# Other orders within even and odd groups, other bank holding times, and one more rounding on the scalar engine in a fused attention and expert-routing kernel

## The reference

```python
xn = _layernorm(x)
# attention: h = rmsnorm(xn) * scale
q, k, v = (einsum("bsd,dhe->bshe", h, w) for w in (wq, wk, wv))
weights = softmax(einsum("bqhd,bkhd->bhqk", q * 64**-0.5, k))
attn = einsum("bqhe,hed->bqd", einsum("bhqk,bkhd->bqhd", weights, v), w_out) + b_out
# experts
logits = silu(xn @ rw1 + rb1) @ rw2 + rb2          # 512 hidden, 8 experts
k_prob = softmax(top_2(logits))
for e in range(8):
    ffn += we[:, None] * (silu(xn @ w1[e] + b1[e]) @ w2[e] + b2[e])
out = x + attn + ffn
```

## Time and profile before

| | |
|---|---|
| median of 3 runs | 2175.5 us (2175.19 to 2176.46) |
| the profiled execution | 2178.22 us, of which the span from first to last instruction is 2176.4 us |
| PE, DVE, ACT, POOL busy in the span | 92%, 75%, 71%, 43% |
| mean granted TensorE clock | 0.965 |

### The profile page before, as it was taken

How to read it: one execution, slowest core, us unless ns; L and a number is a source line. 1 busy time by engine, 2 the same in 40 slices (tenths; PEclk the granted TensorE clock), 3 DMA queues, 4 the chain that set the end, 5 groups by cost and what they waited for, 6 DMA issues and landing times.

```text
span 2176.4 us, 45192 instructions
## 1 busy us (share of the span) xinstructions
PE 2000.1 (92%) x16646; PEld 1285.2 (59%) x16646; DVE 1628.4 (75%) x2716; ACT 1547.2 (71%) x3654; POOL 945.7 (43%) x790
## 2 busy tenths in 40 slices
PE   7898999989998888999889999999999999999997
PEld 5555555555655555565456666666666666666664
DVE  6777777777876677777667877777877877778785
ACT  5667677766766676676567677777777777777774
POOL 4333454443334443332114544645546445464454
PEclk9999999999999999999999999999999999999999
DMA  2122222221011101101213333433333333333332
GB/s 79 37 62 82 80 96 81 77 71 38 28 37 39 35 27 40 39 22 36 84 51 84 70 84 80 79 80 79 87 77 71 88 78 77 80 79 81 75 74 45
DMA packets 132697, 141.96 MB, mean 65 GB/s; under 512 B 25438, under 2 KB 99038, under 8 KB 132446
## 3 DMA queue, kind: packets, MB, share of 16 engines
q1 hardware_dynamic: 101886, 118.34, 17.4%
q0 software_dynamic: 30592, 20.73, 8.0%
HBM read 102.65 MB, written 38.46 MB: 65 GB/s over the span
## 4 chain that ended last, share of the span: by engine, by line
PE 65%; ACT 11%; DVE 11%; issue 7%; another core or an unknown queue 4%; DMA 1%; POOL 0%; SPq 0%; DVEq 0%; POOLq 0%; ACTq 0%
PE pair L452 17%; PE pair L393 12%; PE pair L423 9%; PE pair L237 7%; PE pair L239 5%; PE pair L238 5%; DVE NM L402 4%; ACT PR L408 3%; DVE ZZ L772 2%; PE pair L498 2%; PE pair L500 2%; ACT ZZ L763 1%; DVE PT L438 1%; ACT PT L435 1%
## 5 line engine op out<-in xcount | busy, mean ns | idle before, releaser
L408 ACT ACTIVATE PR<-pair,NM 128x512 f32<-128x512 f32 x1024 | 710.1, 715 | 54.9 <-DVE NM L402 54.3
L402 DVE TENSOR_REDUCE NM<-pair 128x2 f32<-128x1024 f32 x512 | 610.0, 1211 | 72.5 <-PE pair L393 52.9
L435 ACT COPY PT<-pair 128x512 f32<-128x512 f32 x640 | 357.3, 605 | 370.2 <-PE pair L423 348.1
L393 PE MATMUL pair<-KS,QS 64*128 64x512 f32 x3072 | 507.4, 432 | 77.4 <-DVE KS L378 44.5
L452 PE MATMUL pair<-PT,V 128*64 128x512 f32 x2048 | 476.7, 608 | 5.3 <-ACT PR L408 5.3
L423 PEld LDWEIGHTS pair<-idn,PR 64*128 64x128 f32 x8192 | 348.2, 143 | 143.6 <-issue 33.5
L393 PEld LDWEIGHTS pair<-KS,QS 64*128 64x128 f32 x3072 | 267.1, 192 | 251.9 <-issue 155.7
L423 PE MATMUL pair<-idn,PR 64*128 64x64 f32 x8192 | 354.7, 227 | 56.2 <-ACT HS L557 18.2
L778 POOL TENSOR_TENSOR HH<-ZZ,HH 128x512 fp32r<-128x512 f32 x156 | 226.3, 1493 | 322.9 <-DVE HH L777 166.0
L813 POOL DMA_INDIRECT out<-YS,IDW x156 | 245.7, 1575 | 176.3 <-DVE YS L805 119.3
L452 PEld LDWEIGHTS pair<-PT,V 128*64 128x64 f32 x2048 | 137.8, 139 | 274.8 <-issue 255.7
(11 more groups left out here) (168 smaller groups left out, 2866.7 us busy)
## 6 DMA issues: line engine op xcount, KB each, us to landing
E<-w_tab SPq DMA_DIRECT2D x78, 512.0 KB
RB<-l_rows SPq DMA_DIRECT2D x127, 256.0 KB
XG<-slots SPq DMA_DIRECT2D x39, 264.0 KB, 6.3
w_tab<-SPL SPq DMA_DIRECT2D x16, 512.0 KB, 4.3
l_rows<-RT SPq DMA_DIRECT2D x508, 1.0 KB
xin<-in_x SPq DMA_DIRECT2D x16, 256.0 KB, 7.6
XQ<-in_x SPq DMA_DIRECT2D x16, 256.0 KB, 6.4
RAW<-in_w SPq DMA_DIRECT2D x16, 256.0 KB, 7.7
```

The source lines that it names most:

```text
L393: m = e.matmul(bank[bk + j], a[half[j], cols], c[half[j], :], start=(k == 0), stop=(k == 2))
L402: add("dve", lambda e: e.tensor_reduce(NM[:, 2 * t:2 * t + 2], both[:], AX.X, ALU.max, negate=True), needs=[("S", n, t), *([("exp", n - 1, ...
L408: add("act", lambda e: e.activation(PR[:, k, :], bank[bk], ACT.Exp, bias=NM[:, k:k + 1], accum_out=RS[:, n % 2, j, t:t + 1]), needs=[("max ...
L435: add("act", lambda e, r=r: e.copy(dst[r], src[r]), needs=[("T", n, t), *old], name=("PT", n, t, r), place=f"turn{t % 2}")
```

## The change

Nothing is computed otherwise. Orders, engines, distances and holding times change:

```diff
 PE_ORDER = [
-    "S0 T0 S1 T1 inverse kq spread attend ahead weighted experts route".split(),
-    "S0 T0 S1 spread T1 kq ahead attend experts route inverse weighted".split(),
+    "S0 T0 S1 T1 kq spread attend inverse ahead experts weighted route".split(),
+    "S0 T0 S1 ahead spread T1 kq attend route experts weighted inverse".split(),
 ]
 DVE_ORDER = [
-    "inverse max0 turn0 max1 turn1 low values sums side".split(),
-    "max0 turn0 max1 inverse turn1 sums values low side".split(),
+    "inverse turn0 max0 max1 turn1 low values sums side".split(),
+    "max0 max1 turn1 sums values turn0 inverse low side".split(),
 ]
 ACT_ORDER = [
-    "turn0 exp00 exp01 turn1 high exp10 exp11 values hi side".split(),
-    "turn0 exp00 exp01 high values turn1 exp10 exp11 hi side".split(),
+    "turn0 exp00 exp01 turn1 high exp10 exp11 values side hi".split(),
+    "turn0 exp00 exp01 high turn1 exp10 values side exp11 hi".split(),
 ]
-VALUES_ON = [["dve", "act", "act", "act"], ["dve", "act", "act", "act"]]
-HIGH_ON = ["dve", "dve", "dve", "act"]
+VALUES_ON = [["dve", "act", "act", "act"], ["act", "dve", "act", "act"]]
+HIGH_ON = ["act", "dve", "dve", "act"]
 PLAN = {
-    -5: [("rows",)],
-    -3: [("turn",), ("in",)],
+    -7: [("rows",)],
+    -3: [("in",), ("turn",)],
 HOLD = {
-    "S0": (0.9, 4.6), "S1": (0.7, 6.2), "T": (0.5, 2.5), "kq": (0.8, 1.8), "V": (0.8, 2.2), "PV": (3.6, 1.7),
-    "R": (0.2, 2.3), "OP": (1.7, 0.5), "h1": (0.8, 4.3), "w2": (2.9, 1.9), "xg": (0.5, 3.9), "yT": (0.6, 5.1),
-    "r1": (0.8, 3.7), "hT": (0.6, 0.4), "xT": (0.5, 5.2), "oT": (0.5, 2.6), "other": (0.9, 1.3),
+    "S0": (0.9, 5.2), "S1": (0.7, 6.2), "T": (0.5, 3.1), "kq": (0.8, 1.5), "V": (0.8, 2.2), "PV": (3.6, 2.0),
+    "R": (0.2, 0.1), "OP": (1.7, 1.1), "h1": (0.8, 3.1), "w2": (2.9, 1.9), "xg": (0.5, 3.9), "yT": (0.6, 4.5),
+    "r1": (0.8, 2.5), "hT": (0.6, 1.6), "xT": (0.5, 3.4), "oT": (0.5, 1.4), "other": (0.9, 1.0),
 }
```

## The result

The changed kernel takes 2153.34 us (median of 4 runs, 2150.58 to 2157.29), the kernel before took 2175.35 us beside it. The ratio is 0.9897 (95% interval 0.9884 to 0.991): 22.0 us, or 1.0%, faster. The direction was right and the gain nearly four times the 5.8 us of the sum. The profiled execution took 2157.29 us, its span is 2155.5 us.

A forecast was written before the change was run, and what follows sets the result against it. PE, busy for 92% of the span, was taken to bound the kernel, leaving only its idle stretches to shorten. Terms -4.4 - 5.4 + 4.0 = -5.8 us took 2175.5 to 2169.7 us; range 2159 to 2181.

The forecast's parts named there:

- Step 1: Experts' part: one rounding per tile from DVE to ACT speeds DVE's other two; -4.4 and -5.4 us, against +4.0 us.
- Step 3: Bank holding times, routing and experts' parts: changed bank inheritance costs or gains 0 us, experts' bounds -4 and +6.
- 9 waits x 0.6: Behind odd heavy groups: exponentials and K's low part come 0.6 us earlier, shortening PE's waits for KS; -5.4 us.
- 4 x 1.1: Behind even heavy groups: maxima start 1.1 us earlier, shortening PE's 4 waits for PR; -4.4 us.
- The price: Behind even heavy groups: ACT's T0 copies come 0.62 us later, PE's query projection waits some 0.25 us in 16 groups; +4.0 us.
- rival D: Experts' part: earlier maxima move ACT's next group, so OT and QS waits go too; 2160.5 us, chance 0.14.
- Rival A: Behind heavy groups: GpSimd's burst of lo's holds up DVE's s(3), making OT late for PE; 2191 us, chance 0.10.
- B: Behind even heavy groups: ACT is the bound, PE takes the full 0.62 us in all 20; 2178 us, chance 0.17.
- C: Odd groups: PV's matmuls hide the DVE gain, only the 4 PR waits go, against 4.0 of cost; 2175 us, chance 0.17.
- Steps 2 and 4: ACT's exp11 behind "side" in odd groups: 0 us, at most +9.5; rows fetched two groups earlier: 0 us, up to +4.
- step 5: A V copy changes engines with its neighbour in 16 groups, both done in the same group either way; 0 us.
- within the 2 us: Sign that the forecast is right: the routing part stays within 2 us of before.

The follow-up runs named there:

- high: Kernel before with only the first rounding moved from DVE to ACT and "hi" behind "side" on ACT: 2042.07 us against 2057.19, ratio 0.9926.
- quiet: Kernel before with all roundings left on DVE, GpSimd's first three lo's waiting for the third rounding: 2042.18 us, ratio 0.9929.
- best: Changed kernel with the rows' distance back at -5 and exp11 again ahead of "side": 2155.12 us, ratio 0.9904 to the kernel before.
- late: As best, but ACT's first rounding at the end of the next group, all four lo's behind it: 2142.83 us, ratio 0.9851 to the kernel before.
- hold: Kernel before with only the new table of holding times (HOLD): 2051.95 us, ratio 0.9976.
- rows: Kernel before with only the experts' rows fetched at distance -7 instead of -5: 2058.62 us, ratio 1.0011.
- exp11: Kernel before with only exp11 placed behind "side" on ACT in odd groups: 2057.72 us, ratio 1.0006.
- yt51: Changed kernel with yT's holding time put back from 4.5 to 5.1: 2156.99 us against 2176.12 for the kernel before, ratio 0.9909.

## Why the prediction was right in direction and too small

Two steps failed. Step 1 gave nothing to the groups two behind a heavy one, where 4.5 us were gained and where the shorter waits for OT gave 1.8 more. Step 3 put the banks at 0, and the holding times alone measured -5.2 us.

**The mechanism of step 1 held right behind the heavy groups**, with some luck in its numbers. Behind odd heavy groups 9 waits x 0.6 = 5.4 us were forecast and 5.4 measured, but as seven waits that lost 0.8 each: the other two of the nine waits for KS had been 0.4 us long and stayed so. Behind even heavy ones: forecast 4 x 1.1, measured 1.1 in four groups and 0.5 in one. The price was over-sized: 4.0 us forecast, some 2.4 measured in high (0.1 to 0.2 in most of the others, 0.4 in one), since the wait of the earlier trace rows's projection became 0.19 us and not 0.25 and not in all. quiet has -0.1 where high has +0.2, so the added cast costs PE up to 0.3 us in such a group. And DVE's relief was put at 2.3 us a tile, 90 us in all, as if both later roundings were slow in every tile; in the kernel before 64 of the 117 took over 1 us, not 78, and DVE lost 66 us.

**What the step missed is that a late engine stays late for more than one group.** My terms looked at the groups right behind a heavy one and gave nothing to those two behind; the table puts 4.5 us there for odd ones, as eight groups of 0.5 to 0.6 (nine in high, before the 3.3 of G = 215 are taken off). In nine of those groups PE's projection waited for ACT's copy of T0. That is also why the waits for PT didn't grow: these went as those of 0.19 us came. The kernel before, on that level:
```profile
1464.48 0.69 PE L424 MATMUL pair<-idn,PR 64*128 64x64 f32 x16
1465.56 0.50 PE L238 MATMUL pair<-HT,WQ 128*128 128x512 f32 x1 [0.40 <-ACT PT L436]
```
From 1464.48 to 1465.56 are 1.08 us, and with the roundings alone changed (high) the same pair is 0.60 apart:
```profile
1455.44 0.66 PE L423 MATMUL pair<-idn,PR 64*128 64x64 f32 x16
1456.04 0.50 PE L237 MATMUL pair<-HT,WQ 128*128 128x512 f32 x1
```
This is rival D in small: not other waits of the earlier trace rows, but one that I hadn't listed.

**A wait for OT costs more than its length.** The earlier trace rows has three of up to 1.9 us, and I priced such a wait at its own length and left all three as they were. In each of the three groups (G = 152, 200, 248) more than the wait is lost: with a wait of 1.62 us and the clock at 1.00, best took 7.61 us for G = 152, and late, run beside it without that wait, 5.35. And TensorE's clock can fall behind it. In the kernel before on that level, PE in G = 200:
```profile
1546.97 0.71 PE L424 MATMUL pair<-idn,PR 64*128 64x64 f32 x16 [1.90 <-DVE OT L459]
...
1548.88 0.63 PE L239 MATMUL pair<-WV,HT 128*128 128x512 f32 x1
1549.31 0.63 PE L240 MATMUL pair<-WV,HT 128*128 128x512 f32 x1
```
Matmuls of 0.63 us instead of 0.39. The granted clock of that stretch, eighth number, is 0.53, the lower level (1.2 GHz); in high, after a wait of 1.64 us, the same stretch has 1.00:
```profile
1548.40:1552.00 3.60, 3.60 (x13) 2.62 (x11) 2.90 (x4) 3.59 (x10) 0.00 (x0) 0.53 0.05 13
```
```profile
1538.20:1540.60 2.40, 2.26 (x11) 1.36 (x9) 2.40 (x4) 2.38 (x6) 0.00 (x0) 1.00 0.01 1
```
Behind waits of 1.87 to 1.96 us such a group took 8.9 to 9.0 us where the clock fell and 7.9 to 8.0 where it didn't: 1.0 us. The wait alone doesn't decide it. Over thirteen traces the clock fell behind 14 of 20 waits of 1.87 to 2.12 us and behind 4 of 18 of 1.58 to 1.70; hold, whose roundings are those of the kernel before, has it at G = 200 and 248 where the kernel before has it at 152 and 200. In high two of three places lost the lower clock. In the whole change on that level one lost it and one got it, so of its -1.8 us the shorter waits make 1.0 (2.11, 1.90 and 1.88 us became 1.63, 1.62 and 1.61) and the clock nothing that can be told; on the first chip three places became one. Only late removes all three waits: 2.3, 3.4 and 2.3 us shorter than in the changed kernel.

**Step 3 was wrong.** I priced the banks at 0 (bounds -4 and +6) because no row showed a wait. In 15 odd heavy groups T1 came 0.2 us later than it had to, and 13 of these groups were some 0.25 us longer for it (one 0.8, one not at all): 4.1 of the 4.8 us that these groups lost in hold (G = 249, which keeps its bank, has the other 0.7, and has them in rows and exp11 as well). The trace doesn't list it as a wait: the transposes' start slides behind the matmuls before them. Kernel before, then hold:
```profile
1070.23 0.96 PE L394 MATMUL pair<-KS,QS 64*128 64x512 f32 x6
1071.21 0.71 PE L424 MATMUL pair<-idn,PR 64*128 64x64 f32 x16
```
```profile
1069.32 0.95 PE L393 MATMUL pair<-KS,QS 64*128 64x512 f32 x6
1070.08 0.68 PE L423 MATMUL pair<-idn,PR 64*128 64x64 f32 x16
```
0.98 us from the scores' start to T1's, and 0.76. In the kernel before, on that level, this distance is 0.96 to 1.01 us in the 18 groups with the inheritance and 0.77 in G = 141 without it; in hold it is 0.77 or 0.78 in 15 of them and stays at 0.96 to 0.99 in G = 189, 225 and 249. The planner's arithmetic had named 17 places (15 of them in odd heavy groups), and the number to give them was this distance, against that of a group with another bank, not the list of waits. hold and yt51, group by group, show that the cause is this one inheritance.

**Rival A** didn't occur in the changed kernel beyond the three places where it was already: s(3) beside the burst took 0.94 us. **B** is false by the 0.19 us wait. **C** is false, since the waits for KS fell from 9.3 to 3.9 us. Steps 2 and 4 were right within 1.4 us, step 5 as far as the sum of the parts can tell, and the routing part changed by 2.4 us in sum on the first chip, 1.3 on the other, within the 2 us or nearly.

**Whose gain it is.** The prediction described the change as a rounding given to ACT. quiet shows that moving it is not what helps: with nothing moved, -14.4 us; with as much work moved but GpSimd silent for only one of the two roundings left, -4.8. The Trainium skill, page "GPSIMD Engine Reference", section "Key points", says that GpSimd contends with VectorE's instructions in a two-port mode or with two SBUF inputs. The rows agree: the cast takes 0.43 or 1.39 us, s 0.68 or up to 5.29, and the maxima, which read PSUM, have a median of 1.22 us each in the kernel before, beside GpSimd's tensor operations as without them. Which of the two conditions the cast meets, no row shows.

In sum, for G = 137 to 254 of the whole change: -5.5 and -2.6 us were foreseen (as -5.4 and -0.4), -4.5 is the carry into the second group, -1.8 the shorter waits for OT and what follows them, -5.3 stands in the odd heavy groups (-4.1 of it in the 15 with the bank), +0.4 and -0.5 are even heavy groups and G = 137: -19.8. All of these but the first two I had put at 0.

## What to carry to other kernels

Before moving work between engines, see whether the slow instances of an instruction coincide with another engine's: here it was enough to let GpSimd begin when VectorE was through with its casts, in one burst that ends ahead of the next product with two SBUF inputs. Price a delay by the distance between fixed points of neighbouring groups, over two groups or more, not by the list of waits alone: that list left out 4 us in 15 groups and what is lost behind a wait of 1.6 to 1.9 us. Where each part of a change can be built alone, take each one alone: two of these parts brought everything, and what one of them did could be had without its price on ACT.

## What the runs showed of the hardware that I had not expected

The same kernel takes 2175 to 2176 us in the first comparison and beside the last four runs, and 2057 on the two chips of the other eight, with 1.2 us between their traces in the experts' part (G = 137 to 254): a cycle of 8 groups of the routing part takes 61 to 65 us on the slower level and 55 to 57 on the faster. In most cycles, on the slower level, beside the eight scatters by GpSimd (line 664), DVE and ACT both stand still for 3 to 6 us with nothing inside the core that releases them, and PE with them; its next matmuls run at the lower clock. Kernel before:
```profile
607.44 1.29 DVE L438 COPY PT<-pair 128x512 f32<-128x512 f32 x2 [5.49 <-remote]
607.49 0.59 ACT L377 CAST KS<-pair 128x512 fp32r<-128x512 f32 x1 [5.13 <-remote]
...
608.88 1.65 PE L393 MATMUL pair<-KS,QS 64*128 64x512 f32 x6 [4.25 <-DVE PT L438]
```
Six score matmuls take 1.65 us there instead of 0.94, at a granted clock of 0.50. Why only some chips do this was not tried and stays open. It doesn't touch the comparison, since the ratios are each taken on one chip.
